# A mixture-of-experts / attention kernel on one core: three weight loads reordered, the router's logits computed with tokens on partitions, the weights' sum taken from the gathered row

## The reference

```
x = x + 0.5 * moe(layernorm(x))      # 64 experts, 8 chosen per token
x = x + attention(layernorm(x))      # 16 heads of 128, 4 key/value heads, 256 keys per sequence
x = x + 0.5 * moe(layernorm(x))      # the same weights again
```

## Time and profile before

| What | Value |
|---|---|
| Median of 3 runs | 706.43 us (705.62 to 706.86) |
| The profiled execution's own time | 707.37 us |
| Its span, first to last instruction | 705.6 us |
| Mean granted PE clock | 0.963 |
| PE / DVE / ACT / POOL busy | 90% / 71% / 53% / 6% of the span |
| DMA traffic | 62.55 MB, mean 89 GB/s |

### The profile page before, as it was taken

How to read it: one execution, slowest core, us unless ns; L and a number is a source line. 1 busy time by engine, 2 the same in 40 slices (tenths; PEclk the granted TensorE clock), 3 DMA queues, 4 the chain that set the end, 5 groups by cost and what they waited for, 6 DMA issues and landing times.

```text
span 705.6 us, 12277 instructions
## 1 busy us (share of the span) xinstructions
PE 637.0 (90%) x4666; PEld 545.1 (77%) x4666; DVE 502.6 (71%) x1282; ACT 375.9 (53%) x1021; POOL 45.7 (6%) x59
## 2 busy tenths in 40 slices
PE   6738978899999999999999999999999999776995
PEld 5435656689988979999897999989799998545774
DVE  6734544688998768788777877877777778785442
ACT  1503446466766565666565656665556566341341
POOL 2114300000000000000000000000000000024210
PEclk9778989999999999999999999999999999988998
DMA  9978990000000000000000000000000016386971
GB/s 319 347 203 311 405 320 4 1 1 1 1 1 2 1 0 1 1 1 1 1 1 1 1 0 1 1 2 1 1 1 2 1 45 254 136 286 151 406 285 47
DMA packets 27134, 62.55 MB, mean 89 GB/s; under 512 B 6880, under 2 KB 17120, under 8 KB 26816
## 3 DMA queue, kind: packets, MB, share of 16 engines
q1 hardware_dynamic: 25008, 55.94, 22.9%
q0 software_dynamic: 1632, 5.39, 2.3%
q10 hardware_dynamic: 432, 0.39, 0.2%
HBM read 54.36 MB, written 7.36 MB: 87 GB/s over the span
## 4 chain that ended last, share of the span: by engine, by line
PE 74%; DVE 10%; DMA 5%; ACT 5%; issue 3%; POOL 1%; SPq 0%; DVEq 0%
PE bank L1256 18%; PE bank L1258 18%; PE bank L1257 18%; PE bank L1308 8%; PE bank L1093 4%; DMA wq_raw<-wq_in 2%; PE bank L1132 2%; DMA slots<-token_table,slot_index 2%; PE bank L1142 2%; POOL slots L503 1%; PE bank L1077 1%; DMA x<-x_in 1%; PE bank L1064 1%; PE bank L1176 1%; PE bank L1154 1%
## 5 line engine op out<-in xcount | busy, mean ns | idle before, releaser
L646 ACT ACTIVATE probs<-bank,negmax 128x256 f32<-128x256 f32 x256 | 121.6, 495 | 0.0
L659 ACT CAST probsT_hi<-bank 128x512 fp32r<-128x512 f32 x128 | 68.8, 590 | 81.8 <-PE bank L1308 81.8
L976 DVE TENSOR_REDUCE negmax<-bank 128x2 f32<-128x512 f32 x128 | 81.9, 681 | 2.2 <-PE bank L1258 2.2
L1008 DVE TENSOR_TENSOR probsT_lo<-bank,probsT_hi 128x512 fp32r<-128x512 f32 x128 | 81.9, 681 | 1.2 <-ACT probsT_hi L659 1.2
L629 ACT ACTIVATE o_hi<-bank,bv 128x512 fp32r<-128x512 f32 x64 | 44.2, 690 | 64.2 <-PE bank L1258 64.2
L1256 PE MATMUL bank<-k_hi,q_hi 128*128 128x256 f32 x256 | 73.0, 285 | 2.9 <-DVE q_lo L962 2.9
L984 DVE TENSOR_SCALAR probs<-probs,rowinv 128x256 f32<-128x256 f32 x256 | 73.1, 350 | 2.3
L1256 PE MATMUL bank<-o_hi,wo_hi 128*128 128x256 f32 x256 | 72.6, 284 | 1.6 <-DVE o_lo L962 1.6
L962 DVE SCALAR_TENSOR_TENSOR o_lo<-bank,bv,o_hi 128x512 fp32r<-128x512 f32 x64 | 48.0, 750 | 35.7 <-ACT o_hi L629 35.6
L1258 PE MATMUL bank<-k_hi,q_lo 128*128 128x256 f32 x256 | 72.9, 285 | 0.0
L1257 PE MATMUL bank<-k_lo,q_hi 128*128 128x256 f32 x256 | 72.9, 285 | 0.0
(11 more groups left out here) (174 smaller groups left out, 1337.0 us busy)
## 6 DMA issues: line engine op xcount, KB each, us to landing
up_r<-up_in SPq DMA_DIRECT2D x16, 768.0 KB, 11.4
down_r<-down_in SPq DMA_DIRECT2D x14, 512.0 KB, 12.0
up_q<-up_in SPq DMA_DIRECT2D x8, 768.0 KB, 9.0
up_o<-up_in SPq DMA_DIRECT2D x6, 768.0 KB, 8.5
down_q<-down_in SPq DMA_DIRECT2D x8, 512.0 KB, 9.9
token_table<-xn SPq DMA_DIRECT2D x16, 256.0 KB, 12.0
down_o<-down_in SPq DMA_DIRECT2D x6, 512.0 KB, 10.9
x<-x_in SPq DMA_DIRECT2D x4, 512.0 KB, 5.6
```

The lines of the kernel that those rows point to most:

```text
L646: nc.scalar.activation(probs[:, n % 2, t, :], scores_ps[head][:, qt * S:qt * S + S], ACT.Exp, bias=negmax[:, n % 2, t:t + 1], accum_out=ro ...
L659: nc.scalar.copy(probsT[0][:, head].rearrange("p c s -> p (c s)"), probsT_ps[head][:]).then_inc(probsT_high, 1)
L976: nc.vector.reduce_max(negmax[:, n % 2, 2 * head:2 * head + 2], scores_ps[head][:].rearrange("p (t s) -> p t s", t=2), AX.X, negate=True). ...
L1008: nc.vector.tensor_tensor(probsT[1][:, head].rearrange("p c s -> p (c s)"), probsT_ps[head][:], probsT[0][:, head].rearrange("p c s -> p ( ...
```

## The change

- **Loads.** `wv` is now loaded right behind `wk`, and both halves of `wq` stand together behind group 12, ahead of groups 13 to 15. The list `splits` puts V before Q0, so that Q0 is split in steps 13 and 14 instead of 11 and 12.
- **Logits.** `experts_of`, `logitsT` and its copies and transposes are gone. `logits_of(n)` holds 128 tokens still and streams the router's 64 columns, two matmuls for each of four tiles, and leaves tokens on partitions. ACT copies once.
- **Sum of the weights.** `exp8` and the extra column are gone, and `ROW` is 320. In each expert step DVE sums the gathered row's 64 weights, takes the reciprocal, and multiplies by it; the factor 0.5 sits in `quadrant`.
- **The largest token.** DVE's `value_load(limit)` moves from the end of a layer to the end of step 3.
- **Entry to the attention.** `xn4_ready` is raised tile by tile and PE's first transposes wait tile by tile. Two of ACT's four splits before the first copy move behind the second and third copy.
- **Small ones.** 48 instead of 24 matmuls warm PE up at the start. `code_ident` is made before the copies of the tokens; in layer 1 it waits for `y_ready`. The table's last row has ones where the weights stand.

```diff
-ROW = D + E + 1
+ROW = D + E
...
-        splits = columns_of(wk_loaded, wk_raw, wk, 0, 1.0) + q_splits[0] + columns_of(wv_loaded, wv_raw, wv, 0, 1.0)
+        splits = columns_of(wk_loaded, wk_raw, wk, 0, 1.0) + columns_of(wv_loaded, wv_raw, wv, 0, 1.0) + q_splits[0]
...
-        K_SPLIT, V_SPLIT, Q_SPLIT, O_SPLIT = 2, 6, [4, 8, 12, 16], [10, 14, 18, 20]
-        SPLIT_AT = 9
+        K_SPLIT, V_SPLIT, Q_SPLIT, O_SPLIT = 2, 4, [6, 8, 12, 16], [10, 14, 18, 20]
+        SPLIT_AT, SPLIT_EARLY = 9, 6
...
             sp.dma_start(wk_raw[:], wk_in.rearrange("(k p) n -> p k n", p=P)).then_inc(wk_loaded, 16)
+            sp.dma_start(wv_raw[:], wv_in.rearrange("(k p) n -> p k n", p=P)).then_inc(wv_loaded, 16)
+            load_when_free(0, AHEAD)
             for n in range(KD):
-                load_when_free(0, AHEAD + n)
                 sp.dma_start(wq_raw[:, n, :], wq_in[n * P:n * P + P, :]).then_inc(wq_loaded, 16)
-            load_when_free(0, AHEAD + 2)
-            sp.dma_start(wv_raw[:], wv_in.rearrange("(k p) n -> p k n", p=P)).then_inc(wv_loaded, 16)
-            load_when_free(0, AHEAD + 3)
+            for g in range(AHEAD + 1, GROUPS):
+                load_when_free(0, g)
...
-                pool.wait_ge(exps, exp_seen.add(2))
+                pool.wait_ge(exps, exp_seen.add())
...
-                nc.scalar.activation(exp8[:], exp8[:], ACT.Exp).then_inc(exps, 1)
...
             warm(ACT.Exp)
-            for n in range(8, 12):
+            for n in range(8, 10):
                 split_high(n)
             act.wait_ge(bq_scaled, 1)
             for n, job in enumerate(first_fills):
                 take_fill(*job)
+                if 1 <= n < 3:
+                    split_high(n + 9)
...
-                    tie(nc.vector.scalar_tensor_tensor(weight4[:, parity, :], slots[:, u, s + D:D + E:GROUPS], slots[:, u, D + E:ROW],
+                    tie(nc.vector.tensor_reduce(total[:, 0:1], slots[:, u, D:ROW], AX.X, ALU.add))
+                    tie(nc.vector.reciprocal(total[:, 1:2], total[:, 0:1]))
+                    tie(nc.vector.scalar_tensor_tensor(weight4[:, parity, :], slots[:, u, s + D:ROW:GROUPS], total[:, 1:2],
                                                        quadrant[:], ALU.mult, ALU.mult))
...
-                dve.wait_ge(exps, 2 * layer + 1)
-                tie(nc.vector.tensor_reduce(wsum[:, 0, :], exp8[:], AX.X, ALU.add))
-                tie(nc.vector.reciprocal(wsum[:, 1, :], wsum[:, 0, :]))
-                nc.vector.tensor_scalar(expw[:, :, E], wsum[:, 1, :], 0.5, None, ALU.mult).then_inc(winv_ready, 1)
...
                 for s in range(1, GROUPS + 1):
                     slot_step(layer, s, s % 2)
+                    if s == 3:
+                        dve.wait_ge(limit_ready, layer + 1)
+                        most = nc.vector.value_load(limit[0:1, 0:1], min_val=0, max_val=T)
...
-                dve.wait_ge(limit_ready, layer + 1)
-                most = nc.vector.value_load(limit[0:1, 0:1], min_val=0, max_val=T)
...
-                def experts_of(n):
+                def logits_of(n):
 
                     pe.wait_ge(xnT_ready, 8 * layer + 2 * n + 2)
-                    for kd in range(KD):
-                        for pair in range(2):
-                            last = mm(bank[3 + n % 2][E * pair:E * pair + E, 0:2 * P], router_w[:, kd, :],
-                                      xnT[:, (2 * n + pair) % 4, :, kd, :], start=kd == 0, stop=kd == KD - 1,
-                                      tile_position=(0, E * pair))
-                    last.then_inc(logitsT_raw, 1)
...
                     if n >= 2:
                         pe.wait_ge(logits_ready, 4 * layer + n - 1)
-                    for t in range(2):
-                        last = nc.tensor.transpose(bank[(2, 5)[n % 2]][:, t * P:t * P + P], logitsT[:, n % 2, t * P:t * P + P], ident[:])
+                    for t in range(4):
+                        for kd in range(KD):
+                            last = mm(bank[3 + n % 2][:, E * t:E * t + E], xnT[:, (2 * n + t // 2) % 4, t % 2, kd, :],
+                                      router_w[:, kd, :], start=kd == 0, stop=kd == KD - 1)
                     last.then_inc(logits_raw, 1)
...
             pe.wait_ge(constants, 2)
-            for _ in range(24):
+            for _ in range(48):
                 mm(bank[3][:, 0:P], ident[:], ident[:], start=True, stop=True)
...
                     for t in range(4):
+                        if issued.turn is None and uses[0] == 1:
+                            pe.wait_ge(xn4_ready, t + 1)
                         last = nc.tensor.transpose(ps[:, t * P:t * P + P], xn4[:, t, n * P:n * P + P], ident[:])
```

More of the change, by code:

```diff
@@ L150, in macaron_kernel @@
                 chosen = sb(router, "chosen", [P, TILES // 2, 2, E], f32r)
-                expw = sb(router, "expw", [P, TILES, E + 1])
-                wsum = sb(router, "wsum", [P, 2, TILES])
-                exp8 = sb(router, "exp8", [P, TILES, 8])
+                expw = sb(router, "expw", [P, TILES, E])
                 key_i32 = sb(router, "key_i32", [P, FIRST[1]], i32)
@@ L176, in macaron_kernel @@
                 weight4 = sb(experts, "weight4", [P, 2, EG])
+                total = sb(experts, "total", [P, 2])
                 y_parts = sb(experts, "y_parts", [P, GROUPS, 2, D], f32r)
@@ L531, in slot_step @@
                                    bank[0][:, 0:KD * P]).then_inc(slotsT_ready, 1)
-                if layer == 0 and SPLIT_AT <= s < SPLIT_AT + V_SPLIT:
+                if layer == 0 and SPLIT_AT <= s < SPLIT_AT + SPLIT_EARLY:
                     split_high(s - SPLIT_AT)
@@ L556, in copy_tokens @@
                     nc.scalar.copy(xnT[:, u % 4].rearrange("p t k c -> p (t k c)"), bank[u % 2][:]).then_inc(xnT_ready, 1)
-                def copy_expert_major(n):
-                    act.wait_ge(logitsT_raw, logitsT_seen.add())
-                    nc.scalar.copy(logitsT[:, n % 2, :], bank[3 + n % 2][:, 0:2 * P]).then_inc(logitsT_ready, 1)
                 def copy_logits(n):
                     act.wait_ge(logits_raw, logits_seen.add())
-                    nc.scalar.copy(logits[:, 4 * n:4 * n + 4, :].rearrange("p (r t) e -> p t r e", r=2),
-                                   bank[(2, 5)[n % 2]][:, 0:4 * E].rearrange("p (t r e) -> p t r e", t=2, r=2)).then_inc(logits_ready, 1)
-                for u in range(3):
-                    copy_tokens(u)
+                    nc.scalar.copy(logits[:, 4 * n:4 * n + 4, :].rearrange("p t e -> p (t e)"),
+                                   bank[3 + n % 2][:, 0:4 * E]).then_inc(logits_ready, 1)
+                if layer == 1:
+                    act.wait_ge(y_ready, 2 * BLOCKS)
                 for n in range(PARTS):
@@ L571, in expert_layer @@
                                          scale=2.0 ** (PARTS - 1 - n) / CODES).then_inc(code_ready, 1)
-                for n in range(3):
-                    copy_expert_major(n)
-                    copy_tokens(2 * n + 3)
-                    if n > 0:
-                        copy_logits(n - 1)
+                for u in range(3):
+                    copy_tokens(u)
+                for n in range(4):
+                    copy_logits(n)
+                    if n < 3:
+                        copy_tokens(2 * n + 3)
                     if n < 2:
                         copy_tokens(2 * n + 4)
-                copy_expert_major(3)
-                copy_logits(2)
-                copy_logits(3)
-                act.wait_ge(shifted8, layer + 1)
-                nc.scalar.activation(exp8[:], exp8[:], ACT.Exp).then_inc(exps, 1)
                 act.wait_ge(shifted, shift_seen.add())
-                nc.scalar.activation(expw[:, :, 0:E], expw[:, :, 0:E], ACT.Exp).then_inc(exps, 1)
+                nc.scalar.activation(expw[:], expw[:], ACT.Exp).then_inc(exps, 1)
                 warm(ACT.Silu)
@@ L705, in _ @@
             for j in range(EG):
-                last = nc.vector.memset(quadrant[32 * j:32 * j + 32, j:j + 1], 1.0)
+                last = nc.vector.memset(quadrant[32 * j:32 * j + 32, j:j + 1], 0.5)
             tie(last)
@@ L779, in slot_step @@
                         nc.vector.tensor_scalar(bq[:], bq[:], SCALE, None, ALU.mult).then_inc(bq_scaled, 1)
-                    if layer == 0 and SPLIT_AT < s <= SPLIT_AT + V_SPLIT:
+                    if layer == 0 and SPLIT_AT < s <= SPLIT_AT + SPLIT_EARLY:
                         split_low(s - SPLIT_AT - 1)
@@ L798, in expert_layer @@
                     dve.wait_ge(top8_ready, 4 * layer + n + 1)
-                    if n == 3:
-                        nc.vector.tensor_tensor(exp8[:], top8[:], top8[:, :, 0:1].to_broadcast([P, TILES, 8]),
-                                                ALU.subtract).then_inc(shifted8, 1)
                     for a in range(4 * n, 4 * n + 4):
@@ L948, in normalise_tokens @@
                     a = i * 4 + t
```

(7 more changed lines are left out.)

30 lines of the change are left out of this document (10 added, 20 removed).

## The result

Four runs of the changed kernel had a median of 696.94 us (695.15 to 697.86), four of the kernel before 706.64. The ratio is 0.986, with a 95% interval of 0.9836 to 0.9884: 1.4% faster, 9.7 us by the medians. The forecast was 697.3 in a range of 691.5 to 702.5, from a saving of 9.15 us. The sum came out right. The rest of this document is about whether its terms did. Two of them did not, and they missed in opposite directions.

The account below looks back on a forecast made before the run. PE was taken as the bound nearly throughout, with 7.9 us lost in layer 0 to a queued load. Savings of 3.9 + 2.0 + 1.05 + 2.2 = 9.15 from 706.43 gave 697.3 us, range 691.5 to 702.5.

Parts of the forecast that it names:

- A: Layer 0's expert steps: reordered loads turn ACT's stall into three short PE waits; step 15 begins 3.9 us earlier (3.1 to 4.7).
- B: Layer 0's first gather: aligned table rows and weight pieces shorten the store queue; 2.0 us taken, between nothing and 4.8.
- the full 4.8: Layer 0's first gather, if alignment is the reason: 3.2 us from token rows plus half as much again from `expw` stores.
- C: Entry to the attention: two of ACT's `wq_hi` splits move behind later copies, saving 1.05 us (0.5 to 1.5).
- D: Layer 1's routing: new logits and no `wsum` chain bring its first gather 2.2 us earlier (0.5 to 3.0).
- The logits' 1.3: Layer 1's routing: the new logits path saves 1.3 of the 1.8 us that DVE waited for logits.
- The `wsum` chain's 0.8: Layer 1's routing: dropping DVE's `wsum` chain brings `keys` forward by 0.86 us, of which 0.8 was taken.
- E: Every expert step: DVE's added reduce and reciprocal, 0.45 us together, are covered by the gather's spare time and cost nothing.
- The alignment rule in full: Rival, chance 0.24: alignment gives 4.8 us at layer 0's first gather and 3.0 in layer 1's routing; time 693.7 us.
- `wo` too early: Rival, chance 0.12: in layer 0 `wo`'s pieces run beside groups 14 and 15, landing group 15 late; time 703.6 us.
- The gathers as the bound: Rival, chance 0.04: in layer 0 PE waits for gathered rows because `weight_ready` is 0.45 us later; time 709.9 us.

Follow-up runs that it names:

- the repeated run: The changed kernel run again with no edit: median 699.08 us, ratio 0.9864 to the kernel before in the same session.

## Why the prediction was right in sum, and where not

- **A, the loads' order (3.9).** The mechanism was right: the stall comes back as waits for the experts' own weights, and step 15 began 49.25 us after the first gather (49.69 in the repeated run) for 49.4 forecast. The size was not, as a term of this sum. Alone it is worth 3.1 (0.9 to 3.8); beside the rest of the change 0.5 to 2.4 by the stages of single executions, and nothing that the ratios show. The step that failed is the one that priced A on the kernel before and then added the rest: of the 3.6 to 4.0 us by which step 15 came nearer to the first gather, 53.29 - 51.78 = 1.5 are there with the old order too. Also missing in it was the clock behind the waits. A smaller slip: group 13 has 1,280 KB, 512 of them down weights, and not 1,152; only group 15's are 384. Its half 1 of `wq` would have been due at 89.9 instead of 90.2, and nothing follows from that.
- **B, the first gather (2.0, a little under half of 4.8).** The failed step is the halving. The rates of the earlier trace rows were the right evidence and were discounted; the full 4.8 was nearer: 5.3 in the first profile, 3.9 in the experiment that undoes alignment alone. The packets say the same. Over 16 engines, 2,048 token rows at 74.5 ns in layer 0 of the kernel before and 46.6 in the changed one differ by 3.6 us (3.2 forecast), and the pieces of `expw` at 33.6 and 17.7 ns by 2.0 (1.6 forecast). The Trainium skill's rule, which the forecast put behind this rival, has only the direction: an estimate from it is 12% for such rows, where the two rates differ by 55%. That the list and the logits were hidden was right before the change: with the new logits alone the list came 7.6 us later and the gather 0.5. Now the list is only 2.7 ahead of the gather, and the 24 more matmuls help instead of being hidden.
- **C, the entry (1.05).** 13.08 to 12.04, so 1.04. From the last sums' `keep_busy` to the first `k` matmul it is 9.22 us in the kernel before, 9.23 in the one with the new loads alone, and 8.18 and 8.19 in the changed one.
- **D, layer 1's routing (2.2).** The gather came 2.6 earlier, for other reasons. The logits' 1.3 was 0.1. The failed step looked at the wait only: it bounded a new group at 1.9 us (it took 2.0) and never set that against the old one's 5.9 / 4 = 1.5. The `wsum` chain's 0.8 was 1.2. Between `keys` and the list 0.3 is lost again (9.6 before, 9.9 after; not explained), so the list is 33.31 - 32.29 = 1.0 earlier against `yT`. Then 1.56 more came because the gather no longer waits for the table; that is alignment again.
- **E, the sum in each step (0).** Right, and tested with double the work.
- **The rivals.** The alignment rule in full (0.24) was the true one for B and D, but the time that it gave, 693.7, was too low, since A and the logits gave less. `wo` too early (0.12) did not happen in that size: group 15's last piece landed 73.06 + 21.9 = 95.0, just ahead of its use. Some mixing there was: by the DMA records `wo`'s first 1 KB piece ended at 91.2 us, nearly 3 ahead of group 15's last. The gathers as the bound: none waited long enough to show.

The parts as measured: alignment 5.2 (a difference of two medians, with about 2.0 of it in layer 1), the rest of the routing 0.55, the entry 1.04, the loads 0.5 to 2.4. That is 7.3 to 9.2 of the 9.7. The remainder is within the 2 us by which the stages vary from run to run, and isn't assigned. So the total was right by luck: an oversized A and an undersized B cancelled.

## What to carry to other kernels

Before halving a price for lack of proof, ask what else the two rows could differ in: here the two rates of 1 KB rows were nearly the whole answer. Two edits that work on the same full queue need not add up, so price the second one on the kernel that the first one leaves. And where bytes ahead of a load set its landing, don't only reorder: load the part that is wanted soon and leave the rest behind, which here was worth more than the reordering and cost two more DMAs. And where an experiment shows no difference, look in its trace for what hid one: here a full queue hid 7.6 us of slower logits.

## What the runs showed of the hardware

- A store of a 1 KB row into the table in HBM took 46 to 47 ns of a DMA engine where rows start at a multiple of 256 bytes, 47 to 48 at 128, 50 at 64, and 55 to 71 at 4 (59 to 75 in the kernel before). A piece of 256 bytes took 16 to 18 ns, one of 260 at 4-byte starts 29 to 34.
- A float32 matmul record with 64 streamed columns and a new set of 128 x 128 weights took as long (0.123 us) as one with 128 (0.117).
- 24 matmuls more at the start moved the first logits from 3.51 to 1.94 us: the granted clock behind them was 1.00 instead of 0.50.
- Two kernels had 2.1 to 2.2 us of idle issue on PE at the entry, with the same instructions there as the others, which had none. Its cause is open.
